# A ring of 16 places for routed tokens, and a butterfly cut into single steps, in an eight-stage gated layer kernel

## What is computed

```
x = x + tanh(g_xattn[2]) * L2_attention(layernorm(x), ctx, ctx)
# L2_ffn: routes = argmax(softmax(t @ switch_w + switch_b)), p = its probability
#   y = p * (gelu(t @ w1[route] + b1[route]) @ w2[route] + b2[route])
x = x + tanh(g_ffn[2]) * L2_ffn(layernorm(x))
x = x + tanh(g_xattn[3]) * L3_attention(layernorm(x), ctx, mask)     # causal, 16 heads
# L3_ffn: h = butterfly(x @ W_exp + b_exp, up_weights, 512); h = gelu(h + up_bias)
#   h = butterfly(h, down_weights, 512); y = h @ W_con + b_con + down_bias
x = x + tanh(g_ffn[3]) * L3_ffn(layernorm(x))

def butterfly(y, weights, dim):            # 9 stages, pairs (i, i + s), s = 2 ** stage
    for stage in range(weights.shape[0]):
        a, b = halves of y at distance s
        na  = w[..., 0, 0] * a + w[..., 0, 1] * b
        nb2 = w[..., 1, 0] * a + w[..., 1, 1] * b
```

## Time and profile before

| | |
|---|---|
| median of 3 runs | 1550.47 us (1541.92 to 1552.64) |
| profiled execution | 1539.75 us, span 1537.5 us |
| mean granted TensorE clock | 0.828 of full |
| PE busy | 1047.4 us (68%) |
| DVE busy | 940.0 us (61%) |
| ACT busy | 681.6 us (44%) |
| POOL busy | 268.5 us (17%) |

### The profile page before, as it was taken

The page is one execution under the profiler, slowest core; times in us unless marked ns, Lnnn a source line. Parts: engine busy times, 40 slices in busy tenths (PEclk is TensorE's granted clock), DMA queues, the critical chain, the costliest instruction groups (busy, mean ns, idle before and its releaser), DMA issues.

```text
span 1537.5 us, 27823 instructions
## 1 busy us (share of the span) xinstructions
PE 1047.4 (68%) x8534; PEld 579.5 (38%) x8534; DVE 940.0 (61%) x2571; ACT 681.6 (44%) x1465; POOL 268.5 (17%) x398
## 2 busy tenths in 40 slices
PE   1847777765664766886667644990046888888889
PEld 0623343332352332343333223770012333333379
DVE  3826776758988993675555413557954555555344
ACT  0215554537754664574444322550022455443356
POOL 2220000000000000012221223448999000000000
PEclk9958999985787675898888856995556999999989
DMA  7272555339991000000000001214112000000001
GB/s 189 82 62 22 40 39 41 28 61 210 166 165 63 1 1 0 2 1 8 8 8 5 10 9 39 58 53 115 55 67 70 1 1 1 1 1 1 1 19 36
DMA packets 285143, 66.91 MB, mean 44 GB/s; under 512 B 206113, under 2 KB 277857, under 8 KB 285026
## 3 DMA queue, kind: packets, MB, share of 16 engines
q1 hardware_dynamic: 271968, 48.40, 21.5%
q0 software_dynamic: 4896, 14.18, 2.8%
q10 hardware_dynamic: 8162, 2.80, 0.8%
HBM read 34.80 MB, written 30.56 MB: 43 GB/s over the span
## 4 chain that ended last, share of the span: by engine, by line
PE 47%; DVE 29%; issue 12%; ACT 4%; DMA 4%; POOL 2%; ACTq 2%; DVEq 1%; SPq 0%; POOLq 0%
PE bank L972 14%; PE bank L999 4%; DVE x L1696 4%; DVE nmax L1383 4%; PE bank L965 3%; PE bank L975 2%; PE bank L1227 2%; PE bank L1212 2%; PE bank L968 2%; DVE small L1557 2%; PE bank L1257 2%; PE bank L1265 2%; PE bank L983 2%; POOL expert_rows L603 2%; PE bank L1045 2%
## 5 line engine op out<-in xcount | busy, mean ns | idle before, releaser
L1383 DVE TENSOR_REDUCE nmax<-bank 128x8 f32<-128x1024 f32 x192 | 235.1, 1225 | 257.8 <-PE bank L975 257.8
L697 ACT ACTIVATE probs_space<-bank 128x1024 f32<-128x1024 f32 x192 | 196.6, 1024 | 330.8 <-PE bank L983 330.7
L972 PE MATMUL bank<-q_one,k_all 32*128 32x512 f32 x768 | 236.3, 686 | 39.7 <-ACT probs_space L697 22.1
L975 PE MATMUL bank<-k_one,q_all 32*128 32x512 f32 x768 | 245.0, 714 | 5.2 <-ACT k_one L705 3.4
L571 POOL TENSOR_TENSOR var_b<-stats 128x4 f32<-128x4 f32 x8 | 1.6, 204 | 731.3 <-DVE stats L1294 731.3
L999 PE MATMUL bank<-probs_space,vals 128*32 128x128 f32 x3072 | 128.9, 288 | 0.1
L999 PEld LDWEIGHTS bank<-probs_space,vals 128*32 128x32 f32 x3072 | 74.8, 112 | 130.9 <-issue 130.1
L1424 DVE TENSOR_TENSOR nmax_one<-bank,max_row 128x512 bf16<-128x512 bf16 x96 | 66.3, 691 | 60.7 <-PE bank L1034 60.5
L972 PEld LDWEIGHTS bank<-q_one,k_all 32*128 32x128 f32 x768 | 65.7, 195 | 96.0 <-issue 94.9
L1062 PE MATMUL bank<-ident,xn_quad 128*128 128x128 f32 x96 | 17.5, 313 | 109.3 <-ACT xn_quad L760 97.0
L983 PE MATMUL bank<-nmax_one,ones_bf 12*128 12x512 bf16 x384 | 81.6, 396 | 0.0
(11 more groups left out here) (273 smaller groups left out, 2318.5 us busy)
## 6 DMA issues: line engine op xcount, KB each, us to landing
expert_rows<-zeros SPq DMA_DIRECT2D x8, 2128.5 KB, 35.4
late<-in_L_ffn_up_weights_dram POOLq DMA_DIRECT2D x9, 512.0 KB, 4.0
late<-_L_ffn_down_weights_dram POOLq DMA_DIRECT2D x9, 512.0 KB, 3.8
q_one<-expert_rows SPq DMA_DIRECT2D x40, 64.5 KB
x<-in_x_dram SPq DMA_DIRECT2D x4, 512.0 KB, 13.2
context<-in_ctx_dram SPq DMA_DIRECT2D x4, 512.0 KB, 10.0
q_scratch<-k_one SPq DMA_DIRECT2D x4, 512.0 KB, 3.3
v_scratch<-moe_w SPq DMA_DIRECT2D x4, 512.0 KB, 4.6
```

Of the source, the lines that this page charges most:

```text
L697: act.activation(probs[:, 2 * g:2 * g + 2, :, :].rearrange("k g i q -> k (g i q)"), bank_pair[1][:, :, :].rearrange("k g f -> k (g f)"), A ...
L972: pe.matmul(bank[2 + s], group(k_all, u, 2 * g + s), group(q_one, u, 2 * g + s), start=not masked, stop=False)
L975: m = pe.matmul(bank[s], group(q_all, v, 2 * f + s), group(k_one, v, 2 * f + s), start=not masked, stop=True)
L1383: dve.tensor_reduce(nmax[:, u % 2, 0, :].rearrange("q (g i) -> q g i", i=HG)[:, 2 * g:2 * g + 2, :], bank_pair[0][:, :, :].rearrange("q g ...
```

## The change

The ring gets 16 places (`ROUTE_RING`), so a quad's places are used again after four quads instead of two, with four semaphores `scattered_0` to `scattered_3`; the tables behind it in `late` move up by 1008 columns. The butterfly's 18 stages of six operations become 108 steps with the same operations in the same order: POOL loads the first two stages' weights after slot store 0, does one step after each of the slot stores 2 to 39 (38 steps), then waits until DVE has added all 32 tiles (`B_res`), and does the other 70. The semaphore `bf_used` is gone; F3 waits for `bf_step`. `slot_x` keeps its eight places.

```diff
+ROUTE_RING = 16
...
-        ring = late[:, 0:RING * RW].rearrange("p (n d) -> p n d", d=RW)
-        at = 1056
+        at = ROUTE_RING * RW
+        ring = late[:, 0:at].rearrange("p (n d) -> p n d", d=RW)
...
                 sp.wait_ge(S("R_slots"), 1)
-                for c in range(2):
-                    sp.wait_ge(S(f"scattered_{c}"), 16 * NT // 2)
+                for c in range(4):
+                    sp.wait_ge(S(f"scattered_{c}"), 16 * NT // 4)
...
-            def butterfly(n):
+            def butterfly_step(k):
+
+                n, i = divmod(k, 6)
                 up = n < STAGES
...
+                if i == 0:
+                    pool.wait_ge(S(f"bf_in{n % 2}"), 16 * (n // 2 + 1))
+                    past(pool, "bf_step", 6 * n)
+                if i < 4:
+                    c = i if up else (0, 2, 1, 3)[i]
+                    weight = wv[:, c].unsqueeze(1).broadcast_to([P, 2, HID // 2 // w_n, w_n]) if up else wv[:, c]
+                    pool.tensor_tensor(tmp(i), half(src, i % 2), weight, ALU.mult).then_inc(S("bf_step"), 1)
                 else:
...
-                pool.tensor_tensor(a_out, tmp(0), tmp(1), ALU.add).then_inc(S("bf_step"), 1)
-                pool.tensor_tensor(b_out, tmp(2), tmp(3), ALU.add).then_inc(S("bf_step"), 1)
-                step = 6 * n + 6
-                pool.wait_ge(S("bf_step"), step)
-                pool.sem_inc(S("bf_used"), 1)
-                if n + 2 < 2 * STAGES:
+                    if i == 4:
+                        pool.wait_ge(S("bf_step"), 6 * n + 4)
+                    first = 2 * (i - 4)
+                    pool.tensor_tensor(half(dst, i - 4), tmp(first), tmp(first + 1), ALU.add).then_inc(S("bf_step"), 1)
+                if i == 5 and n + 2 < 2 * STAGES:
+                    pool.wait_ge(S("bf_step"), 6 * n + 6)
                     butterfly_weights(n + 2)
...
-                    first = c % 2 * QT
-                    past(pool, f"scattered_{c % 2}", 16 * QT * (c // 2))
+                    first = c % 4 * QT
+                    past(pool, f"scattered_{c % 4}", 16 * QT * (c // 4))
...
-                            in_=ring[:, t % RING, :], in_offset=None).then_inc(S(f"scattered_{c % 2}"), 16)
+                            in_=ring[:, t % ROUTE_RING, :], in_offset=None).then_inc(S(f"scattered_{c % 4}"), 16)
...
                         in_=slot_y[:, s_no % 4, :], in_offset=None).then_inc(S(f"G_back{s_no % 4}"), 16)
-                if "F3" in phases:
-                    butterfly_weights(0)
-                    butterfly_weights(1)
-                    for n in range(STAGES):
-                        butterfly(n)
+                    if "F3" in phases and s_no == 0:
+                        butterfly_weights(0)
+                        butterfly_weights(1)
+                    if "F3" in phases and s_no >= 2:
+                        butterfly_step(s_no - 2)
             if "F3" in phases:
-                for n in range(STAGES, 2 * STAGES):
-                    butterfly(n)
+                pool.wait_ge(S("B_res"), NT)
+                for k in range(NS - 2, 12 * STAGES):
+                    butterfly_step(k)
...
-                        past(act, f"scattered_{c % 2}", 16 * QT * (c // 2))
-                        act.activation(ring[:, w % RING, 0:P], tile_of(x, w), ACT.Identity, bias=shift[:, w:w + 1],
+                        past(act, f"scattered_{c % 4}", 16 * QT * (c // 4))
+                        act.activation(ring[:, w % ROUTE_RING, 0:P], tile_of(x, w), ACT.Identity, bias=shift[:, w:w + 1],
...
-                dve.wait_ge(S("bf_used"), 2 * STAGES)
+                dve.wait_ge(S("bf_step"), 12 * STAGES)
```

More of the change, by code:

```diff
@@ L505, in butterfly_weights @@
                                ).then_inc(S(f"bf_in{n % 2}"), 16)
-            def butterfly(n):
+            def butterfly_step(k):
+                n, i = divmod(k, 6)
                 up = n < STAGES
[L509 to L512, removed]
+                w_n = 2 ** (n if up else 2 * STAGES - 1 - n)
+                src, dst = (n % 2, (n + 1) % 2) if up else ((n - STAGES) % 2, (n - STAGES + 1) % 2)
@@ L513, in butterfly @@
                 wv = bf_w[:, n % 2, :].rearrange("p (n s c) -> p c n s", s=w_n, c=4)
[L514 to L527, removed]
-                else:
[L529 to L541, removed]
@@ L542, in butterfly @@
-                for i, (c, d) in enumerate(zip(order, (a_in, b_in, a_in, b_in))):
-                    last = pool.tensor_tensor(tmp(i), d, wgt(c), ALU.mult)
-                    last.then_inc(S("bf_step"), 1)
-                step = 6 * n + 4
-                pool.wait_ge(S("bf_step"), step)
-                pool.tensor_tensor(a_out, tmp(0), tmp(1), ALU.add).then_inc(S("bf_step"), 1)
-                pool.tensor_tensor(b_out, tmp(2), tmp(3), ALU.add).then_inc(S("bf_step"), 1)
-                step = 6 * n + 6
@@ L550, in butterfly, with half, tmp @@
-                pool.wait_ge(S("bf_step"), step)
-                pool.sem_inc(S("bf_used"), 1)
-                if n + 2 < 2 * STAGES:
+                def half(b, h):
+                    if up:
+                        return bf_up[:, b].rearrange("p m (n two s) -> p two m n s", two=2, s=w_n)[:, h]
+                    return bf_dn[:, b].rearrange("p (n two s) -> p two n s", two=2, s=w_n)[:, h]
+                def tmp(j):
+                    if up:
+                        return bf_t[:, j, :].rearrange("p (m n s) -> p m n s", m=2, s=w_n)
+                    return bf_t[:, j, 0:HID // 2].rearrange("p (n s) -> p n s", s=w_n)
@@ L1051, in attention @@
                         past(pe, "R_cnt", (t - R_RANK) // QT + 1)
-                        pe.transpose(bank[7][:, 2 * P:3 * P], ring[:, w % RING, 0:P], ident[:, :]).then_inc(S("R_xt"), 1)
+                        pe.transpose(bank[7][:, 2 * P:3 * P], ring[:, w % ROUTE_RING, 0:P], ident[:, :]).then_inc(S("R_xt"), 1)
                     c = quad(t, 6)
@@ L1235, in _ @@
                 pe.wait_ge(S("t_mx"), 2 * 3 * NT)
-                pe.wait_ge(S("bf_used"), 2 * STAGES)
+                pe.wait_ge(S("bf_step"), 12 * STAGES)
                 for c in range(NC):
```

## The result

| | before | after |
|---|---|---|
| median of 4 executions | 1546.45 us (1541.92 to 1552.64) | 1482.0 us (1472.8 to 1486.12) |
| profiled execution, own time and span | 1539.75, 1537.5 us | 1479.73, 1477.7 us |
| ratio after/before | | 0.957, 95% interval 0.951 to 0.9635 |

Faster by 64 us, inside the range of 1434 to 1494, but 23 us above the 1459 forecast. Later the same kernel, run twice more, gave 1459.1 and 1461.4 us. So there are two things to explain: the terms of the sum, and those 23 us. In what follows a stage's time is read from the one profiled execution of each kernel.

What follows compares the result with a forecast made beforehand. Bounds: ACT's scatter waits in the second attention's ring, and POOL's butterfly beside DVE's second gather. Terms -67 + 20 - 47 + 2 + 1 = -91 us from a median of 1550.47 give 1459 us, range 1434 to 1494.

Steps and rivals of the forecast that it cites:

- ring, tiles 15 to 31: Second attention: ACT's first four waits for scatters go, sixteen tiles run at 27.65 us per four, giving back 49.0 us.
- ring, tail to the last scatter: End of the second attention: the fifth wait's removal gives 13 us, the sixth's only 5.95 because POOL is late next.
- steps between the stores: Slot stores: one butterfly step behind each makes POOL the bound, 2.8 us a slot instead of 2.25, +20 us.
- last store to tile 0 of the fourth attention: DVE's second gather without the butterfly beside it, -47 us, and the norm's chain of statistics beside POOL's steps, +2.
- fourth attention: Butterfly's end moves out by two multiplications, 3.0 us, beside slower tiles: +1 us, at most 3.
- rival 3: Second attention: another wait takes the ring's place, half of 67 us stays lost: 1492 us; chance 0.08.
- Rival 2: Slots: DVE loses a step to the lock in every slot, 4.05 us each, +67: 1506 us; 0.2 with half case.
- Gather and norm: After the last slot store: reloads to statistics chain fall from 71.3 to 24.1 us, -47; norm's ten operations +2.
- the half case of rival 2: DVE loses a step to the lock in half of the slots: 1482 us; chance 0.2 together with the full case.

Runs made afterwards that it cites:

- after's third run: The changed kernel run unchanged a third time, in the third set of experiments: median 1461.4 us, ratio to before 0.942.
- the ring alone: The kernel before with only the ring of 16, the butterfly left whole after the last slot store: 1483.6 us, ratio 0.958.
- the second run: The changed kernel run unchanged once more, in the second set of experiments: median 1459.1 us, ratio to before 0.939.
- paced: The changed kernel with 66, 87 or 108 butterfly steps waiting for the fourth attention's progress: 1465.9, 1468.2 and 1472.9 us.
- a variant: The changed kernel with POOL issuing a quad's scatters one by one, each behind one more normalised tile: 1458.4 us, ratio 0.941.

## Why the prediction was right, and where its terms were off

Measured on after's third run (own time 1469.15, against 1539.75), and where that can't tell, on the ring alone:

| term | forecast | measured |
|---|---|---|
| ring, tiles 15 to 31 | -49 | 159.64 to 110.2: -49.4 |
| ring, tail to the last scatter (13 + 6, less 1 in the rounding to 67) | -18 | 64.5 to 52.1: -12.4; ring alone 44.4: -20.1 |
| steps between the stores | +20 | 83.3 to 112.9: +29.6 (+26.7 in the second run) |
| last store to tile 0 of the fourth attention | -45 | 116.1 to 62.0: -54.1 |
| fourth attention | +1 | 289.4 to 287.4: -2 |
| sum | -91 | -88; medians -96 and -92 |

The two own times differ by 70.6 only, because the profile of before reached the second attention at 606.5 us and this one at 620.8, through stages that no edit touches, and because that attention's tiles 0 to 15 took 106.7 and 109.5 us. The forecast had nothing for these tiles. They took 109.1 to 110.2 us in all profiles with both parts and 107.8 with either alone; why wasn't settled.

**Ring.** The six waits went, no new one came, and rival 3 is dead. The first term was exact, since it was read from the tiles ahead of the first wait. The tail's 13 + 6 missed the clock: behind tile 31 after's rows show 0.54 where the ring alone has 1.00, 15.55 us of PE for 102 instructions against 13.41 for 133.

**Slots.** The term of 2.8 us a slot was mis-sized, +29.6 us for +20. POOL's timelines show the sum itself, and what it left out; first one stage's multiplications in before, then after's third run:

```profile
1049.43 6.87 POOL L543 TENSOR_TENSOR late<-bf_up,late 128x512 f32<-128x512 f32 x4 [3.47 <-DMA late<-in_L_ffn_up_weights_dram]
```

```profile
953.97 1.00 POOL L602 DMA_INDIRECT token_rows<-q_one,slot_row_int  x1 [0.16 <-issue]
955.00 1.57 POOL L532 TENSOR_TENSOR late<-bf_up,late 128x512 f32<-128x512 f32 x1
956.74 1.00 POOL L602 DMA_INDIRECT token_rows<-q_one,slot_row_int  x1 [0.17 <-issue]
...
1016.42 4.79 POOL L537 TENSOR_TENSOR bf_up<-late 128x512 f32<-128x512 f32 x1
```

Of the 0.35 of "issue" half is hidden, about as I had taken, and the pace is 2.7 to 2.8 us in the later stages. But the multiplications of the first two stages take 1.79 us, not 1.5, so the slots there 2.98. Before's trace had shown that: four took 6.87 us in its first stage, 1.72 each, and I had priced the step from a later stage. DVE's operation of 4.42 us, which I had left on the last store, now holds a step, 4.79 us, two stores ahead of the last: 3.5 us more in the slots, and 3.9 less behind them. The rest, some 3 us, is in the first slots, where POOL waits for DVE's L1672, 1.75 us and then about 0.5 each; in the second run it doesn't, and the slots take 110.0 us. Rival 2, 4.05 us a slot, is wrong as a pace, though DVE is held up as it said: L1665 (L1677 before) now takes 1.05 us at the median where it took 0.15, and hides, as predicted, below POOL's pace.

**Gather and norm.** -54 instead of -45: the reloads to the chain fell from 71.3 to 19.4 us in after's profile, not to 24.1, because the first chunk is there after 4.3 us instead of the 6.8 that before showed, and eight L1684 take 2.17 us together, where I had counted eight times 0.335, 2.7. The 3.9 us of the last store are in it. The chain went from 11.3 to 13.6, +2.3 for a forecast of +2.

**Misses that cancel.** Slots +10, gather -9, tail +6, fourth attention -3: the 1459 hit by the reruns owes something to that. And the result's own 1482 has late results in its second attention, 20.4 us in the profiled execution, that no term or rival accounts for, and no run has settled. The cases nearest to it in time, the half case of rival 2 (1482 us) and rival 3 (1492), would have been the wrong reading of it: its slots are those of the reruns, and no wait took the ring's place.

## What to carry to other kernels

Price the moved work of a slow engine by its own time plus what it holds up, and read the second from operations that are on the path: here a step cost 0.6 to 0.8 us between the stores, 0.7 to 0.8 in a row beside an attention and 0.8 paced beside it, so that moving steps from one to the other gained 8 us at most by the medians of one set, and by the stages next to nothing. Next to nothing it cost only where the neighbour was idle, waiting for a DMA. Spreading work that locks a neighbour out can cost more than leaving it in one heap. And run the kernel under study again in every set: a variant beat the recorded time by 24 us, and so, later, did the unchanged kernel, by 23 and 21.

## What the runs showed of the hardware

- Results of PE can reach DVE and ACT up to 2 us after the records show the matmuls done, with the granted clock still at 1.00 in the record; PE then idles 2.5 us and the clock falls to 0.50 (1.2 GHz) for up to 17 us; the stage was 20 us longer in all. The same instructions run without it in other executions. The Trainium skill (TensorE: Matmul & The Clock Gate, Seeing it yourself) cautions that clock events in traces have been seen to be unreliable; no run here can show whether the clock had really fallen before its record.
- A stage that none of the edits touches differs between profiles: tile 0 of the second attention starts between 604.9 and 625.2 us in the twelve of the experiments. One profile's total tells little below 20 us; its stages tell a lot.
- One to five tiles of the fourth attention take 10.3 instead of 8.7 us in nearly every profile, before and after, with a clock of 0.50 for 2 to 4 us of it and nothing on POOL.
- The clock behind tile 31 (0.54 or 1.00 over 16 us) can differ between kernels with the same work there, 52 or 44 us to the last scatter; why wasn't settled.
